# Seven-product output projection by pairs of heads, in a fused attention and FFN layer on one core

## The reference

```
x  = x + attn(layernorm(x)) ;  x = x + ffn(layernorm(x))
attn:  q = rmsnorm(h @ wq_a.T) * w ;  kv_c = rmsnorm(h @ wkv_a.T) * w     # latents 384, 128 (+64 rotary)
       16 heads: scores = (q_nope, rope(q_pe)) . (k_nope, rope(k_pe)) * SCALE
       attn = softmax(scores) ;  out_h = attn @ v_h
       return concat(out_h) @ wo.T
ffn:   down(silu(gate(h)) * up(h)), weights rounded to fp8, with scales    # 512 -> 1536 -> 512
```

## Time and profile before

| | |
|---|---|
| median of 3 runs | 2230.62 us (2229.79 to 2231.48) |
| profiled execution, its span | 2228.8 us |
| TensorE busy | 2205.4 us (99%), 10977 matmuls |
| VectorE busy | 1557.8 us (70%) |
| ScalarE busy | 1066.6 us (48%) |
| GpSimd busy | 1001.5 us (45%) |
| longest wait of TensorE | 10.5 us, once, for the first layer norm |
| all other listed waits of TensorE | 6.8 us in 14 |

### The profile page before, as it was taken

The page is one execution under the profiler, slowest core; times in us unless marked ns, Lnnn a source line. Parts: engine busy times, 40 slices in busy tenths (PEclk is TensorE's granted clock), DMA queues, the critical chain, the costliest instruction groups (busy, mean ns, idle before and its releaser), DMA issues.

```text
span 2228.8 us, 34908 instructions
## 1 busy us (share of the span) xinstructions
PE 2205.4 (99%) x10977; PEld 1026.8 (46%) x10977; DVE 1557.8 (70%) x3227; ACT 1066.6 (48%) x2345; POOL 1001.5 (45%) x688
## 2 busy tenths in 40 slices
PE   7999999999999999999999999999999999999999
PEld 5444544445444454444544445444454445444454
DVE  7888887776477764777648775587755877467773
ACT  6667564554255542555325553355443554345532
POOL 4657465453355524454244642536334363343322
PEclk9999999999999999999999999999999999999999
DMA  7868336562175631756216561365614564145530
GB/s 248 188 124 150 88 71 142 106 124 51 23 151 105 122 53 34 145 105 127 44 43 146 106 121 29 73 123 106 118 25 104 106 115 95 24 104 109 106 65 19
DMA packets 703800, 219.42 MB, mean 98 GB/s; under 512 B 685520, under 2 KB 685776, under 8 KB 702672
## 3 DMA queue, kind: packets, MB, share of 16 engines
q1 hardware_dynamic: 703696, 218.09, 47.7%
HBM read 40.78 MB, written 8.39 MB: 22 GB/s over the span
## 4 chain that ended last, share of the span: by engine, by line
PE 93%; DVE 3%; ACT 1%; DMA 1%; POOL 1%; issue 1%; SPq 0%; DVEq 0%; POOLq 0%
PE bank L853 13%; PE bank L291 11%; PE bank L293 11%; PE bank L292 11%; PE scores L863 7%; PE scores L663 5%; PE scores L293 5%; PE scores L291 5%; PE scores L292 5%; PE bank L674 4%; PE bank L675 4%; PE bank L676 4%; PE scores L660 3%; PE bank L840 1%; PE bank L689 1%; PE scores L557 1%
## 5 line engine op out<-in xcount | busy, mean ns | idle before, releaser
L1716 POOL TENSOR_TENSOR arena<-arena 128x1024 f16<-128x1024 f32 x256 | 545.7, 2132 | 620.3 <-ACT arena L1079 620.3
L1077 ACT ACTIVATE arena<-scores,shift 128x512 f32<-128x512 f32 x512 | 357.5, 698 | 535.0 <-DVE shift L1429 494.8
L1449 DVE SCALAR_TENSOR_TENSOR arena<-bank,rden,arena 128x512 f32<-128x512 f32 x508 | 347.9, 743 | 137.0 <-PE bank L293 137.0
L1427 DVE TENSOR_REDUCE mx<-scores 128x1 f32<-128x512 f32 x512 | 352.5, 689 | 20.5 <-PE scores L293 16.7
L1079 ACT ACTIVATE arena<-scores,shift 128x512 f16<-128x512 f32 x512 | 358.6, 700 | 0.0
L853 PE MATMUL bank<-arena,WFF 128*128 128x512 f16 x1392 | 313.5, 379 | 0.8 <-DVE arena L1601 0.6
L1774 POOL TENSOR_TENSOR arena<-arena 128x512 f16<-128x512 f32 x96 | 114.4, 1191 | 255.6 <-ACT arena L1152 255.6
L853 PEld LDWEIGHTS bank<-arena,WFF 128*128 128x128 f16 x1392 | 135.9, 98 | 164.1 <-DVE arena L1601 2.3
L291 PE MATMUL bank<-WVO,arena 128*128 (+1 forms) x512 | 194.2, 379 | 2.4 <-DVE arena L1222 1.2
L1222 DVE SCALAR_TENSOR_TENSOR arena<-bank,arena 128x512 f16<-128x512 f32 (+1 forms) x263 | 176.2, 670 | 29.1 <-ACT arena L1070 24.4
L663 PE MATMUL scores<-arena 128*128 128x512 f16 x512 | 195.4, 382 | 0.0
(11 more groups left out here) (159 smaller groups left out, 3480.5 us busy)
## 6 DMA issues: line engine op xcount, KB each, us to landing
arena<-arena SPq DMA_TRANSPOSE x712, 3.2
arena<-w_ffn SPq DMA_DIRECT2D x24, 384.0 KB, 3.5
arena<-x SPq DMA_DIRECT2D x8, 1024.0 KB, 5.6
out<-arena SPq DMA_DIRECT2D x32, 256.0 KB, 2.0
arena<-x SPq DMA_DIRECT2D x14, 512.0 KB, 4.4
WVO<-w_o SPq DMA_DIRECT2D x4, 1024.0 KB, 8.2
arena<-w_nope SPq DMA_DIRECT2D x4, 768.0 KB, 9.1
arena<-down_scale SPq DMA_DIRECT2D x8, 256.0 KB, 3.3
```

Source lines behind the costliest of these rows:

```text
L1077: act.activation(P32[:, t, :], SC[:, t, :], ACT.Exp, scale=EXP_SCALE, bias=shift[:, t:t + 1], accum_out=esum[:, par, t:t + 1]).then_inc(s[ ...
L1427: dve.tensor_reduce(mx[:, t:t + 1], SC[:, t, :], AX_X, ALU.max).then_inc(s["mxr"], 1)
L1449: dve.scalar_tensor_tensor(out=XR[:, t, :], in0=banks[t][:, :], scalar=by[:, t:t + 1], in1=XR[:, t, :], op0=ALU.mult, op1=ALU.add).then_in ...
L1716: pool.tensor_tensor(PL[:, par, two, :], P32[:, two, :], PH[:, par, two, :], ALU.subtract).then_inc(s["pl"], 1)
```

## The change

In batches 2 to 7 (`B_PLAIN = 2`), heads 0 to 13 are projected in seven pairs ("duos"); heads 14 and 15 and batches 0 and 1 stay as they were.

- **Seven products.** For a pair, the 4 row tiles in two halves, the two heads and the 512 columns in two halves make a 2x2 by 2x2 block product. It is taken by a scheme with 7 block products in place of 8, with 4 sums of context blocks and 4 of weight blocks. A product is 2 tiles x 3 matmuls of 256 columns (`duo_product`). Products gather in three banks, and VectorE adds 8 half-bank results to `XR` (`ADDS`).
- **Weights.** In batch 1 GpSimd makes the block sums of `WVO`, ScalarE rounds them, and SP writes all 7 blocks of each pair to DRAM (`w_duo`). From batch 2 on, SP loads them pair by pair, 4 blocks (`early_blocks`, 0.5 MB) and 3 blocks (`late_blocks`, 0.4 MB), into space that `WVO` held.
- **Division before rounding.** Sums over two heads need probabilities already divided. ScalarE now takes each exponential once, as float32, waits for VectorE's reciprocals, writes `PH` as a scaled copy of `P32`, and scales `P32` in place; the fourth tile's scaling (in heads 0 to 2 the third's too) is a multiplication on GpSimd.
- **Context halves from the bank.** ScalarE copies the needed context blocks from `BC` (`context_hi`), VectorE takes them as float32 (`context_rows`) and their low halves (`context_lo`), and GpSimd forms the four sums and their two halves.
- **Order.** Values lag by two heads (`values(i-2)` in step i), and a pair's products stand in steps 2j+4 (early) and 2j+5 (late). TensorE's scores wait for `ex` (float32 exponential) in place of `ph`.
- **Input.** From batch 1 on, the rows of the batch after the next are loaded at the end of attention and their statistics and scaling are done by VectorE in the FFN; ScalarE and GpSimd split them in the steps of the next attention. XR is loaded in step 1 in place of step 0.
- In the last FFN, `LAST_DOWNS` finishes tiles 0 to 2 first.

The diff, cut to its core:

```diff
+EARLY = [(X_E1, W_B11, 0, True), (X_O1, W_B21, 2, True), (X_S1, W_T1, 1, True), (X_S2, W_T2, 0, False)]
+LATE = [(X_S3, W_T3, 0, False), (X_S4, W_B22, 1, False), (X_O2, W_T4, 2, True)]
...
@@ sync
+            def duo_head(b, i):
+                if i < NH - 2:
+                    sp.wait_ge(s["sp"], NT * (b * NH + i) + NT)
+                    rope_rows(i + 2, i % 2)
+                if i >= 2:
+                    sp.wait_ge(s["ctp"], b * N_CT + i - 1)
+                    sp.sem_inc(s["turn"])
+                for half in range(2):
+                    prob_rows_hi(b * NH + i, i % 2, half)
+                    prob_rows_lo(b * NH + i, i % 2, half)
...
+                    if not plain:
+                        if i >= 4 and i % 2 == 0:
+                            early_blocks(b, i // 2 - 1)
+                        elif i >= 5:
+                            late_blocks(b, i // 2 - 1)
...
@@ tensor
-                    if not (isinstance(pair, int) and pair == 0 and par == 0):
+                    if b >= B_PLAIN and 0 < pair * 2 + par < NH - 1:
+                        pe.wait_ge(s["ex"], g * NT + (t - NT + 1))
...
+            def duo_product(j, x, w, k, start):
+                for t in range(2):
+                    dst = DBANK[k][:, t * HB:(t + 1) * HB]
+                    for m, (p, q) in enumerate(((0, 0), (0, 1), (1, 0))):
+                        r = pe.matmul(dst, lhsT=XP[j % 2][:, p, x, tile(t)], rhs=WB[:, q, w, :],
+                                      start=(start and t == 0 and m == 0), stop=(m == 2), skip_group_check=True)
+                return r
...
+            def duo_late(b, j):
+                n, base = (b - B_PLAIN) * N_DUO + j + 1, order_of_duo(b, j)
+                pe.wait_ge(s["w_late"], 16 * n)
+                pe.wait_ge(s["outr"], base + 4)
...
+            def duo_step(b, i):
+                scores(b, i // 2, i % 2)
+                if i >= 2:
+                    values(b, i // 2 - 1, i % 2)
+                if i >= 4 and i % 2 == 0:
+                    duo_early(b, (i - 4) // 2, (0,))
+                if i == 5:
+                    duo_early(b, 0, (2, 3))
+                absorb(i + 2, b * NH + i + 2)
+                if i >= 4 and i % 2 == 0:
+                    duo_early(b, (i - 4) // 2, (1,) if i == 4 else (1, 2, 3))
+                elif i >= 5:
+                    duo_late(b, (i - 5) // 2)
...
@@ scalar
+            def probs_divided(b, i):
+                g, par, n = b * NH + i, i % 2, (b - B_PLAIN) * (2 * N_DUO) + i
+                for t in range(NT):
+                    act.wait_ge(s["shift"], NT * g + t + 1)
+                    if i > 0 and t % 2 == 0:
+                        act.wait_ge(s["pl"], 2 * g - 1 + t // 2)
+                    act.activation(P32[:, t, :], SC[:, t, :], ACT.Exp, scale=EXP_SCALE, bias=shift[:, t:t + 1],
+                                   accum_out=esum[:, par, t:t + 1]).then_inc(s["ex"], 1)
+                for t in range(NT):
...
+                    if t == NT - 1 or t == NT - 2 and i < N_TWO:
+                        act.wait_ge(s["nm3"], by_pool(b, i, t))
+                        act.activation(PH[:, par, t, :], P32[:, t, :], ACT.Copy).then_inc(s["ph"], 1)
+                    else:
+                        act.activation(PH[:, par, t, :], P32[:, t, :], ACT.Copy,
+                                       scale=rden_duo[:, par, t:t + 1]).then_inc(s["ph"], 1)
+                        act.activation(P32[:, t, :], P32[:, t, :], ACT.Copy,
+                                       scale=rden_duo[:, par, t:t + 1]).then_inc(s["nm"], 1)
+                    if t == 0 and i >= 2:
+                        context_hi(b, i - 2)
...
@@ vector
+            def duo_step(b, i):
+                g = b * NH + i
+                maxima(g)
+                reciprocals(b, i)
+                if i >= 2:
+                    context_rows(b, i - 2)
+                if i >= 4 and i % 2 == 0:
+                    duo_adds(b, (i - 4) // 2, (0,))
+                if i == 5:
+                    duo_adds(b, 0, (2, 3))
+                if i >= 2:
+                    context_lo(b, i - 2)
+                if i >= 4 and i % 2 == 0:
+                    duo_adds(b, (i - 4) // 2, (1,) if i == 4 else (1, 2, 3))
+                elif i >= 5:
+                    duo_adds(b, (i - 5) // 2, (4, 5, 6, 7))
+                qa_lo(g + 2, i % 2)
...
@@ gpsimd
+            def last_heads(b, i):
+                g, par = b * NH + i, i % 2
+                head(g, par, (0,))
+                if par:
+                    context_sums(b, N_DUO - 1)
+                    context_sums_rest(b, N_DUO - 1)
+                head(g, par, (1,))
```

More of the change, by code:

```diff
@@ L87 @@
 N_ROT_FFN = 5
+NS = 2.0**13
 RSQRT_MAGIC = 0x5F3759DF
@@ L470, in batch @@
                         weight_chunk(c)
+                if not first and not last:
+                    early_blocks(b + 1, 0)
+                    late_blocks(b + 1, 0)
+                    if ahead:
+                        next_input(b + 1)
                 if not last:
@@ L511, in _ @@
             output_matrix(3)
-            batch(0, False, first=True)
-            with sp.Fori(1, B - 1) as b:
+            batch(0, False, first=True, plain=True)
+            batch(1, False, plain=True)
+            with sp.Fori(B_PLAIN, B - 2) as b:
                 batch(b, False)
+            batch(B - 2, False, ahead=False)
             batch(B - 1, True)
@@ L1181, in ffn, with batch @@
                     qa_hi((b + 1) * NH + 1, 1)
-            def batch(b, last, first=False):
-                attention(b, last, first)
+            def batch(b, last, first=False, plain=False):
+                attention(b, last, first, plain)
                 ffn(b, last, first)
@@ L1212, in _ @@
             setup_queries_and_keys()
-            batch(0, False, first=True)
-            with act.Fori(1, B - 1) as b:
+            batch(0, False, first=True, plain=True)
+            batch(1, False, plain=True)
+            with act.Fori(B_PLAIN, B - 1) as b:
                 batch(b, False)
@@ L1642, in ffn @@
                                              op1=ALU.mult).then_inc(s["yt"], 1)
-                if last:
-                    for t in range(2, NT):
+                    if last and t >= 2:
                         dve.wait_ge(s["yt"], b * NT + t + 1)
@@ L1709, in keys_rotated_lo, with head @@
                                    ALU.subtract).then_inc(s["kpl"], 1)
-            def head(g, par):
-                for half in range(2):
+            def head(g, par, halves=range(2)):
+                for half in halves:
                     two = slice(2 * half, 2 * half + 2)
@@ L1746, in attention @@
+            def attention(b, last, first, plain):
                 base = b * NH
@@ L1752, in attention @@
                 for i in range(NH):
-                    head(base + i, i % 2)
-                    if i == 0:
+                    if plain:
+                        head(base + i, i % 2)
+                    elif i < 2 * N_DUO:
+                        head_divided(b, i)
+                    else:
+                        last_heads(b, i)
+                    if plain and not first and i >= 2:
+                        if i % 2 == 0:
+                            block_sums(i // 2 - 1)
+                        else:
+                            block_sums_lo(i // 2 - 1)
+                    if i == 0 and plain:
                         for n in range(N_ROT_FFN + 1, N_ROT):
@@ L1760, in attention @@
                         join_chunk(chunk_of(i - 1))
-                    if 0 <= i - start < NT and not last:
-                        next_norm(b, i - start, stg)
+                    if plain and 0 <= i - start < NT:
+                        if first:
+                            next_norm(b, i - start, stg)
+                        else:
+                            next_rows_lo(b, i - start)
+                    if not plain and not last and i in STG_STEPS:
+                        next_rows_lo(b, STG_STEPS.index(i))
             def ffn(b, last, first):
@@ L1802, in _ @@
             rotate(0, NT)
-            batch(0, False, first=True)
-            with pool.Fori(1, B - 1) as b:
+            batch(0, False, first=True, plain=True)
+            batch(1, False, plain=True)
+            with pool.Fori(B_PLAIN, B - 1) as b:
                 batch(b, False)
```

512 lines of the change are left out of this document (447 added, 65 removed).

## The result

The changed kernel takes 2276.25 us (median of 4, 2268.51 to 2279.61) against 2230.2 before (2229.4 to 2231.48): ratio 1.0198, 95% interval 1.0179 to 1.0218. That is 46 us more where 11 were forecast, and above the upper end of the range, 2260. Its profiled execution (2279.04 us) has a span of 2277.2 us, 48.4 above that of before. The four executions took 2268.51, 2273.46, 2279.04 and 2279.61 us at a mean granted clock of 0.995, 0.993, 0.990 and 0.990: the lower the clock, the longer.

A forecast was written before the change was run, and what follows sets the result against it. TensorE, 100% busy at full clock from 880 to 2120 us, was taken as the bound. 2228.8 - 25 + 19 + 15 + 4.2 - 1.9 - 0.9 = 2239, with 1.8 for the median 2241 us; range 2208 to 2260.

The forecast's parts named there:

- The seven products: TensorE, pairs of heads: 42 half-width matmuls replace 24 full ones, saving 0.60 us a pair, -25 us in all.
- Rival 4: Half-width matmuls cost more than half, deciding from 123 ns on; at 144 ns some 2290 us; chance 0.02.
- rival 3: ScalarE and VectorE set every step, their chain 11.2 us against TensorE's 10.9; 2275 us; chance 0.10.
- ScalarE's and VectorE's chain: One head's work from first maximum to next: 10.1 us (even) or 10.3 (odd), hidden behind TensorE's steps in the steady part.
- The front: First steps of a batch: scores wait for the previous head's exponentials, 3.2 us a batch with later waits, +19 us over six.
- The end: End of attention: late weights of the last pair and a projection wait, +3.0 us a batch, +15; last batch +4.2.
- Last batch: No latents to fill with, so its end waits cost +4.2 us; two earlier waits there go, -1.9.
- tail: Program's end: three of four tiles end early, so one addition no longer follows the last product, -0.9 us.
- Batch 1: Weight block sums made once there by GpSimd, ScalarE and queues idle over a third of a step: 0, bounds -1 and +3.
- Input normalised in the FFN stage: VectorE's added work per chunk hides, the gate's product having more than 1 us to spare: 0, bound +3.
- T2 to T5: Starts of scores in a batch's first steps, over which TensorE's 2.5 us of waiting for exponentials was spread.
- Rival 1: The lag is soaked up and TensorE remains the bound throughout; 2205 us; chance 0.20.
- rival 2: Only the first steps of a batch cost, since the last pair's weights and additions are in time; 2224 us; chance 0.15.

The follow-up runs named there:

- e8: Changed kernel plus matmuls whose results nobody reads, 24 in step 4 and 12 at the last pair's late weights of each batch: 2262.22 us.
- e5: Changed kernel with the edits of e1 and e2, and VectorE's low half of QA behind the next head's maxima in steps 2 to 5: 2241.04 us.
- e9: e5 with the first pair's product from head 1's halves put into the third product's bank, in step 4: 2236.16 us.
- e13: e1 with the other bank of e9 for the first pair's product, without e5's order on VectorE: 2246.04 us.
- e1: Changed kernel with the last pair's late weights issued between the third and fourth transpose of head 15, not behind the fourth: 2257.86 us.
- e11: e10 with GpSimd's weight block sums in batch 1 split, 5 behind each head instead of 10 behind the even one: 2230.45 us, ratio 0.9995.
- e10: e9 with the statistics of the input two batches ahead moved four chunks later in the FFN stage on VectorE: 2232.97 us.
- e2: Changed kernel with the first pair's product from head 1's halves issued one step later, behind head 5's scores, its addition moved alike: 2269.45 us.
- e12: e11 with the first two of a pair's three late products exchanged, and their additions with them: 2223.28 us, ratio 0.9965.

## Why the prediction was wrong, step by step

Against 2241 the result is 35 us too long. The largest single part is a term that the sum put at nothing and gave no reason for: the clock, 14 us (e8). The other 21 are terms that were too small, so that even e8, at the full clock, is at 2262, over the range's upper end of 2260.

- **The seven products, -25.** Right: 109 ns, 25.4 us. Rival 4, half-width matmuls, is refuted by the 109 ns, and rival 3, a chain that sets every step, by the steady steps of 11.25 and 10.60 us.
- **ScalarE's and VectorE's chain, 10.1 and 10.3.** Right or slightly high. Scaled copies are 0.61 to 0.62 apart (taken 0.62), GpSimd's multiplication 1.04 (1.23); heads' exponentials start 8.6 to 9.9 us apart in the front, forecast 9.15 to 10.3. Head 4's first maximum is 40.2 us behind the batch's first scores, forecast 41.7.
- **The front, +19.** Mechanism right, place wrong, size low. The steps exceed their natural lengths by 0.6 (step 2) and 3.5 (step 4), 4.1 us a batch, 25 in all. The chain was even a little faster than forecast and cost more all the same: I followed the scores' wait for the exponentials and not the product's wait for the bank of head 2's context, which falls due later on the same chain. That 19 lies near 25 is in part luck. e5, e9 and e13 show that the chain is the cause: its order on VectorE is worth 1.4 us a batch, the bank 0.7 to 0.8.
- **The end, +15 and +4.2.** Right in mechanism and near in size: weights behind the four transposes, 2.4 to 3.3 us, and 0.40 at the projection, each with the 0.16 of a matmul's end that an idle stretch lays bare: some 18 for five batches. The 1.26 left in e1 is the "about 1" forecast.
- **Last batch, +4.2 - 1.9, and tail, -0.9.** +1.4 in all was forecast, some +6 measured. Waits of 2.82 (weights), 1.16 and 1.09 stand there, and a new one of 1.71 in the tail, for the normalised rows, where I had expected a gain. No run takes the last three away, so why they are there stays open.
- **Batch 1, 0 (bounds -1 and +3).** +4.0: above its bound. I compared GpSimd's busy share with the step and not its order: a pair's 6.6 us of sums stand in one piece between two heads' remainders (e11).
- **Input normalised in the FFN stage, 0 (bound +3).** +3.2, at its bound (0.6 of it lies in batch 1 and is in the 4.0 too). I looked at the gate's product, which indeed doesn't wait; late were the queries' low halves, and so the transposes (e10).
- **The missing term: the clock.** The sum had no term for it. It is 14 us of the 46 (e8). I had the two stalls at about 3 us each and left them at their own length; I had even spread the front over four small waits. The step that failed is "TensorE stands 2.5 us, spread over T2 to T5", and the end's 3.0 taken alone: the runs show one wait of 3.04 us in step 4 and one of 2.4 to 3.3 at the weights, and behind 10 of the 12 the clock at half.

Together, by the spans: -25.4 + 25 + 18 + 6 + 4.0 + 2.6 - 0.6 and 16.6 of clock make 46 of 48.4. Some 2 us are not assigned.

The Trainium skill (TensorE: Matmul & The Clock Gate, "Part 1: The HAM clock gate") says that the array's clock goes by how busy TensorE has lately been, with 1.2 and 2.4 GHz as the only levels. The trace agrees: 0.50 granted behind a stall, and e8 shows that filling the stalls is enough. Held against my own two stalls, that rule gave a rival that I did not list. I had no price for it; with e8's it would have stood at 2241 + 14 = 2255, inside the range and still 21 us short.

The chances: 0.50 stood on slower, and slower it is. Rival 1 (2205) and rival 2 (2224) fell to the rows; rival 3 came near the time, 2275, by a mechanism that is not there, which is luck.

## What to carry to other kernels

A saving on the engine that is 100% busy counts only where the others keep up *in that stretch*: walk the first steps and the last ones of a stage with all waits of every moved instruction, those for a bank to be read out too, and not the averages. A wait of 2 us or more on TensorE cost its length and, at 19 of the 30 such stalls in the profiled executions of the changed kernel, e1, e2 and e13, the clock behind it; if it can't be removed, shorten it (at 1.81 us the clock never fell) or fill it, and price both. Where three engines hand one chain around, pulling one forward shows the next at once: e5's order, e9's bank, e12's exchange had to come together, and the 13 us from e9 to e12 came from single instructions' places.

## What was not expected of the hardware

- The length of a stall doesn't settle whether the clock falls. In one execution it fell at 10 of 12 stalls of 2.4 to 3.3 us, and stayed at 1.00 at one of 3.04 us (batch 4) and one of 2.37 (batch 5). In e1 it fell at 2 of the 6 stalls of 3.03 us in step 4; in e2 it stayed at 1.00 at 3.77 us and fell at 2.60; in e13, with 2.17 us in each batch's step 5, it fell at 2 of 6. What decides is open. It is one reason why like batches differ by 4 us.
- Matmuls that nobody needs, 36 of 0.109 us in each of six batches, made the kernel 14 us faster (0.6%).
- The slow stretch costs less than the windows' clock says: 22 us by (1 - clock) x time, 16.6 by e8, against the same execution of the changed kernel.
